# Flamingo block on one core: the sum of squares of q is formed and read out per pair of heads instead of per four heads

## The reference, cut to what matters

```python
def rmsnorm(x, w, eps=EPS):
    var = jnp.mean(x * x, axis=-1, keepdims=True)
    return w * (x * jax.lax.rsqrt(var + eps))
q = (hidden_states @ q_proj_w.T).reshape(B, Q, NUM_HEADS, HEAD_DIM).transpose(0, 2, 1, 3)
k, v = ...                       # from the context, 8 heads, each repeated 4 times
q, k = rmsnorm(q, q_norm_w), rmsnorm(k, k_norm_w)
scores = jnp.einsum('bhqd,bhkd->bhqk', q, k) / np.sqrt(HEAD_DIM) + attention_mask
out = jnp.einsum('bhqk,bhkd->bhqd', softmax(scores), v)
x = x + tanh(g_xattn[0]) * (out @ o_proj_w.T)
```

## The kernel before, in words

| engine | order within step b (unit offset) |
|---|---|
| PE | scores (0), sum_squares (+4), q_proj (+6), p_transpose (-1), o_proj (-2), values (-1) |
| ACT | oT_split (-2), qT_copy (+5), square (+5), weight copies, exps (0), q_seed (+4), pT_split (-1), v_split (+2) |
| DVE | oT_split (-2), mask_max (0), pick_sums (+4), q_half (+4), p_recip (0), pT_split (-1), accumulate (-2) |
| POOL | weight remainders, q_rstd (+4), v_split (+2), normalize (0) |

## Time and profile before

### The profile page before, as it was taken

How to read it: one execution, slowest core, us unless ns; L and a number is a source line. 1 busy time by engine, 2 the same in 40 slices (tenths; PEclk the granted TensorE clock), 3 DMA queues, 4 the chain that set the end, 5 groups by cost and what they waited for, 6 DMA issues and landing times.

```text
span 787.3 us, 12378 instructions
## 1 busy us (share of the span) xinstructions
PE 747.2 (95%) x3847; PEld 587.2 (75%) x3847; DVE 456.2 (58%) x1006; ACT 431.1 (55%) x1274; POOL 275.2 (35%) x431
## 2 busy tenths in 40 slices
PE   6999989899999999999999999999999988887997
PEld 4788877688887878888878788888787743565775
DVE  4786412456465555564655555655558755887653
ACT  5553315556556556655655655655655557556831
POOL 0331005234325323424423523432322438714242
PEclk9999999999999999999999999999999999997999
DMA  8545461132041140140132203203132135754232
GB/s 303 190 130 174 133 191 42 47 155 81 15 175 31 64 175 28 54 185 16 67 113 88 67 29 161 81 14 122 34 122 96 55 107 167 287 243 151 82 110 78
DMA packets 42126, 87.82 MB, mean 112 GB/s; under 512 B 5561, under 2 KB 26041, under 8 KB 38226
## 3 DMA queue, kind: packets, MB, share of 16 engines
q1 hardware_dynamic: 38884, 78.71, 28.7%
q0 software_dynamic: 3184, 8.41, 3.1%
HBM read 70.28 MB, written 35.57 MB: 134 GB/s over the span
## 4 chain that ended last, share of the span: by engine, by line
PE 69%; DVE 5%; POOL 4%; DMA 3%; ACT 3%; issue 2%; POOLq 0%; SPq 0%; DVEq 0%
PE banks L881 8%; PE banks L883 7%; PE banks L882 7%; PE banks L915 7%; PE banks L917 7%; PE banks L916 7%; PE banks L867 7%; PE banks L902 3%; PE banks L894 2%; PE banks L1829 2%; PE banks L1830 2%; PE banks L1831 2%; PE banks L926 2%; PE banks L928 2%; PE banks L927 2%
## 5 line engine op out<-in xcount | busy, mean ns | idle before, releaser
L592 ACT ACTIVATE p_sb<-p_sb,nmax 128x128 f32<-128x128 f32 x256 | 99.7, 391 | 57.5 <-DVE nmax L784 57.4
L587 ACT ACTIVATE oT_hi<-banks 128x512 fp32r<-128x512 f32 x64 | 38.2, 596 | 135.0 <-PE banks L928 135.0
L821 DVE SCALAR_TENSOR_TENSOR x_sb<-banks,tgates,x_sb 128x512 f32<-128x512 f32 x64 | 47.9, 749 | 65.9 <-PE banks L917 65.9
L690 POOL TENSOR_TENSOR v_lo<-v_raw,v_hi 128x128 fp32r<-128x128 f32 x64 | 29.5, 460 | 127.7 <-ACT v_hi L635 127.7
L779 DVE SCALAR_TENSOR_TENSOR p_sb<-banks,q_rstd,mask 128x128 f32<-128x128 f32 x256 | 71.4, 341 | 2.9 <-POOL q_rstd L83 2.4
L695 POOL TENSOR_TENSOR p_sb<-p_sb,rsum 128x512 f32<-128x512 f32 x64 | 66.5, 1039 | 15.1 <-DVE rsum L811 15.1
L867 PEld LDWEIGHTS banks<-kT,qT_sb 128*128 128x128 f32 x512 | 67.7, 193 | 5.4
L867 PE MATMUL banks<-kT,qT_sb 128*128 128x128 f32 x512 | 68.2, 277 | 0.0
L768 DVE TENSOR_TENSOR oT_lo<-banks,oT_hi 128x512 fp32r<-128x512 f32 x64 | 44.1, 689 | 32.9 <-ACT oT_hi L587 32.9
L400 PE MATMUL banks<-w_hi,ctx_hi 128*128 128x512 f32 x128 | 54.1, 422 | 7.9 <-DVE ctx_lo L331 7.8
L811 DVE RECIPROCAL rsum<-prob_sum 128x4 f32<-128x4 f32 x64 | 11.3, 176 | 81.8 <-ACT p_sb L592 81.8
(11 more groups left out here) (276 smaller groups left out, 1888.7 us busy)
## 6 DMA issues: line engine op xcount, KB each, us to landing
sorted_x<-in_empty SPq DMA_DIRECT2D x8, 2064.0 KB, 11.2
w_raw<-in_wq_l SPq DMA_DIRECT2D x8, 1024.0 KB, 5.9
w_raw<-in_wo_l SPq DMA_DIRECT2D x8, 1024.0 KB, 4.8
exp_w<-in_exp_w_l SPq DMA_DIRECT2D x8, 1024.0 KB, 10.6
kT_scr<-kT_st SPq DMA_DIRECT2D x16, 256.0 KB
v_scr<-v_st SPq DMA_DIRECT2D x16, 256.0 KB, 2.3
xs<-sorted_x SPq DMA_DIRECT2D x15, 258.0 KB, 3.6
v_raw<-v_scr SPq DMA_DIRECT2D x14, 256.0 KB, 2.6
```

What stands on the lines that cost most here:

```text
L592: last = act.activation(p_sb[:, b % 2, h * P:(h + 1) * P], p_sb[:, b % 2, h * P:(h + 1) * P], ACT.Exp, bias=nmax[:, b % 2, h:h + 1], accum ...
```

## The change

The sums are formed after every second head, over two heads: four matmuls of 256 moving columns, a mask product and a reduction of 8 blocks of 32 instead of 16, and the seed still once per half, when both pairs are there. The semaphores `ss_done`, `picked_done` and `sumsq_done` count pairs, 4 per group of heads, in place of halves, 2 per group. `square` of unit u now waits for the pair before the last (the one that held its slot of `sq`), where the first square of a half waited for the sums of the half just before it.

```diff
-        picked = m.sb("picked", [P, HG * HB, ROWS])
+        picked = m.sb("picked", [P, 2 * HB, ROWS])
             def square(u, b, g, odd):
-                reached(act, ss_done, 2 * g + b // HG)
+                reached(act, ss_done, 4 * g + b // 2 - 1)
             def q_seed(u, b, g, odd):
-                act.wait_ge(sumsq_done, 2 * g + c + 1)
+                act.wait_ge(sumsq_done, 4 * g + 2 * c + 2)
             def pick_sums(u, b, g, odd):
-                if h < HG - 1:
+                if h % 2 == 0:
                     return
-                half = 2 * g + c
-                dve.wait_ge(ss_done, half + 1)
-                reached(dve, sumsq_done, half)
-                dve.tensor_tensor(picked[:, :, :], blocks(ss_ps[:, :], HG * HB),
-                                  same[:, :].unsqueeze(1).to_broadcast([P, HG * HB, ROWS]), ALU.mult).then_inc(picked_done, 1)
-                dve.wait_ge(picked_done, half + 1)
-                reached(dve, ln_done, half - 1)
-                dve.tensor_reduce(ss[:, c, :], picked[:, :, :], axis=AX_X, op=ALU.add).then_inc(sumsq_done, 1)
+                pair = 4 * g + b // 2
+                dve.wait_ge(ss_done, pair + 1)
+                reached(dve, sumsq_done, pair)
+                dve.tensor_tensor(picked[:, :, :], blocks(ss_ps[:, 0:2 * HB * ROWS], 2 * HB),
+                                  same[:, :].unsqueeze(1).to_broadcast([P, 2 * HB, ROWS]), ALU.mult).then_inc(picked_done, 1)
+                dve.wait_ge(picked_done, pair + 1)
+                reached(dve, ln_done, 2 * g + c - 1)
+                dve.tensor_reduce(ss[:, c, (h - 1) * HB:(h + 1) * HB], picked[:, :, :], axis=AX_X, op=ALU.add)\
+                    .then_inc(sumsq_done, 1)
             def q_half(u, b, g, odd):
-                dve.wait_ge(sumsq_done, 2 * g + c + 1)
+                dve.wait_ge(sumsq_done, 4 * g + 2 * c + 2)
             def sum_squares(u, b, g, odd):
-                if b % HG < HG - 1:
+                if b % 2 == 0:
                     return
                 pe.wait_ge(squared, u + 1)
                 pe.wait_ge(s.ones_set, 1)
-                reached(pe, picked_done, 2 * g + b // HG)
-                heads = sq.rearrange("p h (b q t) -> p h b q t", q=P // ROWS, t=ROWS)
+                reached(pe, picked_done, 4 * g + b // 2)
+                pair = sq[:, b % HG - 1:b % HG + 1, :].rearrange("p h (b q t) -> p h b q t", q=P // ROWS, t=ROWS)
                 for q in range(P // ROWS):
-                    last = pe.matmul(ss_ps[q * ROWS:(q + 1) * ROWS, :], s.ones[:, 0:ROWS], heads[:, :, :, q, :],
+                    last = pe.matmul(ss_ps[q * ROWS:(q + 1) * ROWS, 0:2 * HB * ROWS], s.ones[:, 0:ROWS], pair[:, :, :, q, :],
                                      start=True, stop=True)
                 last.then_inc(ss_done, 1)
-                    pe.wait_ge(picked_done, UNITS // HG)
+                    pe.wait_ge(picked_done, UNITS // 2)
```

## The result

The changed kernel is slower: the ratio to the kernel before is 1.0075, with a 95% interval of 1.0044 to 1.0104. The median is 797.38 us (5 runs, 793.02 to 799.69) beside 790.42 us of the kernel before (5 runs, 788.69 to 791.25). The forecast was 793.7 us, the range 791.2 to 795.6 us: the direction was right, the time lies above the range.

A forecast was written before the change was run, and what follows sets the result against it. PE, busy without a gap in steps 3 to 57, was taken to bound the kernel; +0.42 (start) + 4.34 (steps 3 to 57) - 0.30 (end) = +4.46 us on 789.23 us gave 793.7 us, range 791.2 to 795.6 us.

The forecast's parts named there:

- What bounds it, and the length of steps 3 to 57: Attention steps 3 to 57: PE never waits, so 28 groups in place of 14 lengthen them by 4.34 us.
- What a group costs: Sums on PE: 1.17 us per group with 512 columns, 0.74 us with 256, of which 0.17 us going in.
- What hides VectorE: DVE's new piece in steps b = 1 and 5, 0.83 us a pair, fits into 1.72 us of idle time.
- The start: Before the attention's steady steps: an added group delays POOL's weights and the first mask_max, +0.42 us, bounds 0 and +0.74.
- The end: Steps 59 and 60: DVE's halved pick lets the last reciprocal start earlier, -0.30 us.
- Rival 1: Step 2: shorter idle time in step 1 keeps PE's clock at 2.4 GHz, 1.53 us come back, 792.2 us; 20%.
- Rivals 2 and 3: Steps 3 to 57: 2, a group costs half, 789.2 us, 12%; 3, DVE's piece too long, PE waits, 800.7 us, 3%.
- The sum and its range: Whole kernel: +4.46 us on the profiled 789.23 us gives 793.7 us, range 791.2 to 795.6 us.

The follow-up runs named there:

- TensorE's part alone: Changed kernel with sums per pair on TensorE kept, but VectorE's product and reduction once per four heads as in the kernel before; ratio 1.0059, median 793.5 us.
- both sets in one step: Kernel before with its group of four 512-column matmuls written as eight of 256 columns, one after the other in the same step; ratio 0.9979.
- VectorE's part alone: Changed kernel with TensorE summing four heads at once as before, VectorE's product and reduction in two pieces of 256 after it; ratio 0.9996.
- its pieces late: Changed kernel with TensorE's sums per pair kept, but both VectorE pieces of 256 after the second pair; ratio 1.0091, median 797.39 us.
- pairs in fp16: Changed kernel with squares and ones kept in fp16; ratio 0.9890, median 781.45 us.
- second and third comparison: Changed kernel, unedited, measured twice more beside the kernel before; ratios 1.0064 and 1.0030, medians 794.29 and 793.07 us.
- the first comparison: Changed kernel against the kernel before, the measurement under The result; ratio 1.0075, median 797.38 us.
- the fp16 kernel: Kernel before, four heads per group, with squares and ones kept in fp16; ratio 0.9832, median 777.02 us; run again 0.9845, 777.92 us.

## Why the prediction was right or wrong

**What bounds it, and the length of steps 3 to 57: right.** +4.34 us forecast, +4.38 us in all three profiles of the changed kernel and in the one with TensorE's part alone.

**What a group costs: right, and for the stated reason.** The table gives a group behind its start, to which 0.17 us of way in comes:

| | 512 columns | 256 columns |
|---|---|---|
| fp32 | 1.00 us | 0.57 us |
| fp16 | 0.33 us | 0.22 us |

Halving the columns takes 0.43 us off in fp32 and 0.11 us in fp16; what is left, if time goes by columns otherwise, is 0.57 - 0.43 = 0.14 us and 0.22 - 0.11 = 0.11 us. With the 0.17 us of way in, 0.28 to 0.31 us of each group is fixed, and 14 added groups at 0.31 us are the 4.34 us. Running both sets in one step removes it. The Trainium skill, TensorEngine Tiling (Array Packing), section Key Properties, says that changing the tiling mode drains TensorE. The runs agree that the change costs, and give its size, 0.3 us in and out together. That a drain is what takes this time no run here shows by itself; the weight loads that start only with their matmul at both changes would fit it.

**What hides VectorE: right.** A piece of the product took 0.42 us against the 0.42 us taken, and in the odd step the reciprocal still waits. These are the rows of DVE that answer to the earlier trace rows, the second with the new piece ahead of it:

```profile
140.54 0.18 DVE L812 RECIPROCAL rsum<-prob_sum 128x4 f32<-128x4 f32 x1 [1.72 <-ACT p_sb L592]
...
144.17 0.18 DVE L812 RECIPROCAL rsum<-prob_sum 128x4 f32<-128x4 f32 x1 [0.93 <-ACT p_sb L592]
```

**The start: a term mis-sized.** +0.42 us was forecast, +0.80 us seen. The path that it named is right: POOL's q_tmp comes 20.91 us after the attention's first matmul where it came 20.46 us, +0.45 us against +0.42 us. But the sum has nothing between q_rstd and mask_max, and there 0.37 us more are lost. The first mask_max starts 0.49 us behind the end of q_rstd, where it had started 0.12 us behind it (the first row is of the kernel before; its mask_max stands in the earlier trace rows):

```profile
134.95 0.22 POOL L83 TENSOR_TENSOR q_rstd<-q_seed,q_tmp 128x16 f32<-128x16 f32 x1
```

```profile
136.27 0.22 POOL L83 TENSOR_TENSOR q_rstd<-q_seed,q_tmp 128x16 f32<-128x16 f32 x1
...
136.98 1.13 DVE L779 SCALAR_TENSOR_TENSOR p_sb<-banks,q_rstd,mask 128x128 f32<-128x128 f32 x4 [4.01 <-POOL q_rstd L83]
```

This is not chance. From the start of q_rstd to that of mask_max it is 0.70 to 0.71 us in all three profiles of the changed kernel and 0.34 to 0.35 us in the nine others, also with TensorE's part alone, with VectorE's part alone, with its pieces late, and with pairs in fp16. What holds it is open. The whole stretch up to step 3 takes 38.5 and 40.1 us in the two profiles of the kernel before, 39.3 to 40.9 us in the three of the changed one; what spreads it is whether one or two stretches at half clock fall into it. With two of them it is 40.10 us against 40.90 and 40.86 us, with one 38.51 against 39.25 us: +0.74 to +0.80 us each time.

**The end: right.** -0.30 us forecast, -0.31 us seen; absent with TensorE's part alone.

**Rival 1 (clock in step 2).** It did not come in any of the three profiles of the changed kernel: the clock fell behind an idle time of 2.05 to 2.06 us, and in the first of them step 2 took 9.00 us. But step 2 ran at full clock in the second profile of the kernel before (7.58 us) after the same 2.44 us idle, and in those of VectorE's part alone (7.60 us) and of the pairs in fp16 (7.53 us). So the kernel before, unchanged, shows both. Rivals 2 and 3 are refuted by the steps of 8.34 us and by PE's gapless stretch.

**The sum and its range: this step failed.** The sentence that the profiled execution "is itself the median of the three runs, so nothing is to be added" treated all that lies outside the change as fixed. It is not. The kernel before alone spreads over 785.56 to 796.01 us in 81 runs on three chips, with a mean of 789.94 us. The median of the changed kernel itself was 797.38 us in five runs and 794.29 and 793.07 us in twelve each. The range was built from uncertainties in the terms of the change (0.67 to 0.80 us a group) and left this out; even with every term at its upper bound, +6.0 for the groups, +0.74 for the start and 0 for the end, the sum would have been 796.0 us.

The 3.7 us between 793.7 and 797.38 us can be traced in part. The sum started from 789.23 us, but the kernel before came out at 790.42 us with two more runs: 1.2 us. The start has 0.4 us more than forecast. And the five runs of the changed kernel spent 27.7 us at half clock on average, where the 81 runs of the kernel before spent 22.9 us: 4.8 us, at some 0.35 us of kernel time for each us, are 1.7 us (an estimate from the slope of the runs below).

What the change itself costs is seen better in the second and third comparison. There the changed kernel has a mean of 794.39 us in 24 runs and the kernel before 790.14 us in the 40 beside them, +4.25 us where the sum had +4.46 us. That it is so near is luck in part: by the profiles the terms are 0.80 + 4.38 - 0.31 = 4.87 us, and the 24 runs had 0.9 us less at half clock than the 40.

From the first comparison 38 single executions of the changed kernel are on record, with a mean of 796.04 us. They spent 26.2 us at half clock against 22.7 us in the 24; at some 0.35 us of kernel time for each us (the slope within the 38), that is 3.5 x 0.35 = 1.2 of the 1.65 us between them. What I can't settle is why the first comparison drew more time at half clock. Two of three profiles of the changed kernel have 10.3 us of it near 675 us behind waits of 3.37 and 3.23 us at L1320. None of the nine other profiles has more than 3.5 us there, among them two with the same steps on TensorE, so this is not nothing. Yet the kernel with late pieces waited 3.40 us in that place and the fp16 kernel 3.09 us, and both kept their full clock. Nor is a low clock reserved to the changed kernel: a mean clock of 0.982 or less, as those two profiled runs have it, is found in 12 of 81 runs of the kernel before, in 5 of the 24 and in 18 of the 38. That the change itself lengthens the time at half clock is neither shown nor wholly excluded; in the two later comparisons the mean is 0.9 us lower with the change.

## What to carry to other kernels

On a TensorE that never waits, count switches of matmul form (how many rows and columns of the array a matmul uses), not only columns: a small group of 128x32 matmuls between 128x128 ones paid 0.3 us per visit here, with 256 columns as with 512, so splitting it in two for an earlier start on engines that are hidden anyway is a loss, while merging visits or cheapening the data type (fp16: 0.50 in place of 1.17 us per group; that kernel is 1.6% faster, and 9.4 of its 12.7 us are these groups) is a gain. Before giving a range, ask how far the rest of the program moves by itself; three runs that agree within 2.6 us hid a spread of 10 us.

## What the runs showed of the hardware that I had not expected

- Eight matmuls of 256 columns in 128x32 form take exactly as long as four of 512, 1.00 us; there was no cost per matmul to be seen, where I had allowed 0.05 us a group.
- The clock level after an idle time of a given length is not the same in every run: after 2.44 us in step 1, step 2 took 9.13 us in one run and 7.58 us in another of the same kernel.
- An engine can stand still in the hardware loop with nothing to wait for that the profile shows: where the loop starts its second pass, in step 24, ACT was idle for 3.85 us in one run and for 2.52 to 2.63 us in the eight other profiles of fp32 kernels.
- At a change of form the weight load of the next matmuls did not run ahead: it started with its first matmul (188.80 us, after 0.41 us idle), where from values to scores, both 128x128, it started 0.23 us ahead.
- Keeping the squares and ones in fp16 also made twelve unrelated matmuls, those of o_proj, 0.04 us shorter per step in all three profiles of fp16 kernels; the reason is open.
